# Moving work across three stage seams of a fused two-layer kernel, and four residual additions from VectorE to GpSimd

## The reference, cut to what matters

```
x = x + selective_scan_layer(ln(x))        # ends in a layernorm of its own, with gain and bias
x = x + fp4_gated_ffn(ln(x))
x = x + linear_attention(ln(x))
x = x + fp4_gated_ffn(ln(x))
x = x + forgetting_attention(ln(x))        # 16 heads of 64, decay = cum[t] - cum[s]
x = x + ln(x) @ sign(W).T
x = x + rope_attention(ln(x))              # 16 heads of 8, q and k rotated and normalised
x = x + ln(x) @ sign(W).T
```

## Time and profile before

| | |
|---|---|
| runs of the kernel before | 2290.7, 2298.5, 2292.94 us; median 2292.94 us |
| the profiled execution | 2297.52 us, its span 2295.7 us |
| mean granted TensorE clock | 0.933 of full speed |
| PE busy | 1917.0 us (84% of the span) |
| DVE busy | 1503.1 us (65%) |
| ACT busy | 1379.4 us (60%) |
| GpSimd busy | 1001.4 us (44%) |
| where the four places stand | `prep` 0 to 21 us, `ln_ssm` 364 to 381, `fg` and the start of `fu` 807 to 860, `rp` and the start of `rt` 1908 to 2010 |

### The profile page before, as it was taken

How to read it: one execution, slowest core, us unless ns; L and a number is a source line. 1 busy time by engine, 2 the same in 40 slices (tenths; PEclk the granted TensorE clock), 3 DMA queues, 4 the chain that set the end, 5 groups by cost and what they waited for, 6 DMA issues and landing times. The chain is left out here.

```text
span 2295.7 us, 36184 instructions
## 1 busy us (share of the span) xinstructions
PE 1917.0 (84%) x11875; PEld 885.0 (39%) x11875; DVE 1503.1 (65%) x2277; ACT 1379.4 (60%) x2289; POOL 1001.4 (44%) x1110
## 2 busy tenths in 40 slices
PE   5468885677968748999999999999999767699997
PEld 2123333444654313444444444444444323222222
DVE  5979995793359667787777787777786437311112
ACT  3557773343344336766776667677665435699994
POOL 0167771560136314656666656566656622300001
PEclk9779998798979869999999999999999979799998
DMA  2000000000000011111111112111111101321210
GB/s 91 0 14 0 0 0 1 0 1 1 0 0 1 0 54 47 51 55 51 55 58 58 55 56 57 50 58 59 58 54 63 38 10 37 101 55 46 52 42 37
DMA packets 71431, 84.47 MB, mean 37 GB/s; under 512 B 20544, under 2 KB 44032, under 8 KB 71168
## 3 DMA queue, kind: packets, MB, share of 16 engines
q1 hardware_dynamic: 66224, 79.80, 11.7%
q10 hardware_dynamic: 5040, 2.56, 0.4%
HBM read 71.95 MB, written 9.57 MB: 36 GB/s over the span
## 5 line engine op out<-in xcount | busy, mean ns | idle before, releaser
L1692 DVE SCALAR_TENSOR_TENSOR fu_kv<-fu_ps_kv,fa_vec,fu_kv 128x511 f32<-128x511 f32 x366 | 252.8, 740 | 6.2 <-ACT fu_kv L1622 5.2
L2089 ACT ACTIVATE rt_p<-rt_ps_s 128x1024 f32<-128x1024 f32 x256 | 240.4, 1042 | 26.2 <-PE rt_ps_o L2034 17.4
L1773 POOL TENSOR_TENSOR fu_p<-fu_p 128x768 f32<-128x768 f32 x64 | 116.8, 1824 | 289.2 <-PE fu_ps_n L1467 284.1
L1437 PE MATMUL fu_ps_s<-fu_qn,fu_kn 64*128 64x512 f32 (+3 forms) x1024 | 190.0, 468 | 12.8 <-DVE fu_sg L1738 6.9
L1672 DVE TENSOR_REDUCE fu_nm<-fu_ps_m 128x2 f32<-128x1024 f32 x64 | 78.4, 1225 | 164.9 <-PE fu_ps_m L1460 164.9
L623 POOL TENSOR_TENSOR scan_hC<-scan_h,scan_c 128x1024 f32<-128x1024 f32 x64 | 150.9, 2357 | 71.5 <-DVE scan_h L599 71.5
L1467 PE MATMUL fu_ps_n<-fu_p,fu_vt 128*64 128x512 f32 (+3 forms) x1024 | 166.1, 445 | 0.0
L599 DVE TENSOR_TENSOR_SCAN scan_h<-scan_dA,scan_ps_b 128x1024 f32<-128x1024 f32 x64 | 146.4, 2287 | 2.2
L522 PE MATMUL scan_ps_y<-scan_hC,w_ident 128*128 128x512 f32 x256 | 125.2, 611 | 27.0 <-POOL scan_hC L623 15.4
L2034 PE MATMUL rt_ps_o<-rt_p,rt_va 128*32 128x512 f32 x1024 | 138.1, 611 | 10.0 <-ACT rt_p L2089 8.1
L1495 PE MATMUL fu_ps_kv<-w_XN,fa_wp 128*128 128x512 f32 x244 | 125.7, 639 | 17.6 <-DVE fu_cr L1665 15.4
(11 more groups left out here) (364 smaller groups left out, 5096.0 us busy)
## 6 DMA issues: line engine op xcount, KB each, us to landing
fu_rb<-rms_rows SPq DMA_DIRECT2D x256, 128.0 KB, 2.9
fu_ro<-rms_rows SPq DMA_DIRECT2D x128, 128.0 KB, 2.9
ra_stackq<-rope_parts SPq DMA_DIRECT2D x168, 32.0 KB
ra_stackk<-rope_parts SPq DMA_DIRECT2D x168, 32.0 KB
w_X<-in_xT SPq DMA_DIRECT2D x4, 512.0 KB
fa_wp<-in_wp SPq DMA_DIRECT2D x8, 256.0 KB
fu_cr<-ncum_rows SPq DMA_DIRECT2D x128, 3.0 KB
rope_parts<-rp_hi SPq DMA_DIRECT2D x16, 128.0 KB, 2.4
```

What stands on the lines that cost most here:

```text
L1437: pe.matmul(sps[:, h, at:at + T - t * P], k[head(h), t * P:(t + 1) * P], q[head(h), t * P:T], start=(at == 0), stop=False)
L1692: dve.scalar_tensor_tensor(acc, projected(a, k)[:, 0:T - j], vec[:, a % GA, at:at + 1], acc, ALU.mult, ALU.add).then_inc(done, 1)
L1773: pool.tensor_tensor(tail, tail, P13[:, :, 0:3 * P], ALU.add).then_inc(s.d1, 1)
L2089: act.activation(pr[k % 2][i][:, :, :], sps[(U * n + u) % RING][:, :, :], ACT.Exp, scale=DH_B ** -0.5).then_inc(s.exp, 1)
```

## The change

- `prep`: the 23 later loads are issued by SP, behind its own nine, and no longer by ACT.
- `ln_ssm`: GpSimd adds the residuals of batches 0 to 3; DVE keeps those of batches 4 to 7, and all eight multiplications.
- `fg` and `fu`: the tiles `nc`, `cr` and `mhl` move to the enclosing stage. The 11 memsets are done by DVE in `fg`, behind that of `ones` and ahead of the gates. SP issues the store of `NC` in `fg` as before and waits for it at the start of `fu`. PE, SP and GpSimd no longer wait for the memsets.
- `rp` and `rt`: for the last two batches (`LATE = 2`) the split into three parts moves from `rp` to `rt`. There DVE makes `HI` and `MID`, GpSimd the differences (behind the copies of `va` for batch 0), and SP puts the 12 pieces in DRAM ahead of its loads for batch 1. The tiles `hi`, `mid`, `lo` and `un` move to the enclosing stage.

```diff
@@ prepare_weights @@
                     sp.dma_start(X[:, b:b + 2, :], w.xT_dram[:, b:b + 2, :]).then_inc(s.x, 16)
+                for src, dst in w.loads:
+                    sp.dma_start(dst, src).then_inc(w.loaded, 16)
...
                     act.dma_start(dst, src).then_inc(w.early, 16)
-                for src, dst in w.loads:
-                    act.dma_start(dst, src).then_inc(w.loaded, 16)
@@ ln_ssm @@
                     for n in range(B):
                         scale(n)
-                        if n:
+                        if n > HALF:
                             add(n - 1)
                     add(B - 1)
+
+                @block.gpsimd
+                def _(pool):
+                    for n in range(HALF):
+                        pool.wait_ge(s.norm, n + 1)
+                        pool.tensor_tensor(X[:, n, :], X[:, n, :], DL[:, n, :], ALU.add).then_inc(s.shared, 1)
+                    pool.wait_ge(s.shared, HALF)
@@ forget_gates @@
-                sp.dma_start(ncum_rows, NC[:, :, :]).then_inc(s.put, 16)
-                sp.wait_ge(s.put, 16)
+                sp.dma_start(ncum_rows, NC[:, :, :]).then_inc(held.stored, 16)
...
                 dve.memset(ones[:, :], 1.0).then_inc(s.ones, 1)
+                for k in range(3):
+                    dve.memset(CR[k][:, :], 0.0).then_inc(s.zero, 1)
+                dve.memset(MHL[:, :, :, :], 0.0).then_inc(s.zero, 1)
+                dve.wait_ge(s.zero, 4)
+                for h in range(2):
+                    for k in range(3):
+                        dve.memset(CR[k][64 * h:64 * h + 5, :], 1.0).then_inc(s.made, 1)
+                dve.memset(MHL[:, :, :, 0:3], 1.0).then_inc(s.made, 1)
@@ forget_units @@
                 sp.wait_ge(held.loaded, 16 * (GA + 2))
-                sp.wait_ge(s.set, 9)
-                sp.wait_ge(s.ones, 6)
+                sp.wait_ge(held.stored, 16)
...
                 pe.wait_ge(held.loaded, 16 * (GA + 2))
-                pe.wait_ge(s.set, 9)
-                pe.wait_ge(s.ones, 6)
@@ rope_project @@
-                for n in range(2, B):
+                for n in range(2, SPLIT):
                     put(n, s.put)
-                sp.wait_ge(s.put, 16 * 6 * (B - 1))
+                sp.wait_ge(s.put, 16 * 6 * (SPLIT - 1))
...
-                    if real(older):
+                    if 0 <= older < SPLIT:
                         act.wait_ge(s.un, older + 1)
...
-                for n in range(B):
+                for n in range(SPLIT):
                     pool.wait_ge(s.hi, n + 1)
@@ rope_attend @@
+                    if n == 0:
+                        for k, m in enumerate(late):
+                            for part, (done, tile) in enumerate(((s.hi, HI), (s.mid, MID), (s.lo, LO))):
+                                sp.wait_ge(done, k + 1)
+                                for j in range(2):
+                                    sp.dma_start(parts_dram[part, j, :, m, :], tile[:, j, m, :]).then_inc(s.put, 16)
+                        return
+                    if n == late[0]:
+                        sp.wait_ge(s.put, 16 * 6 * LATE)
...
+                    if i == 0:
+                        for k, m in enumerate(late):
+                            pool.wait_ge(s.hi, k + 1)
+                            pool.tensor_tensor(rest[k][:, :, :], un[m % 2][:, :, :], HI[:, :, m, :], ALU.subtract).then_inc(s.rest, 1)
+                        for k, m in enumerate(late):
+                            pool.wait_ge(s.mid, k + 1)
+                            pool.tensor_tensor(LO[:, :, m, :], rest[k][:, :, :], MID[:, :, m, :], ALU.subtract).then_inc(s.lo, 1)
...
             @block.vector
             def _(dve):
+                for m in late:
+                    dve.tensor_copy(HI[:, :, m, :], un[m % 2][:, :, :]).then_inc(s.hi, 1)
+                for k, m in enumerate(late):
+                    dve.wait_ge(s.rest, k + 1)
+                    dve.tensor_copy(MID[:, :, m, :], rest[k][:, :, :]).then_inc(s.mid, 1)
```

More of the change, by code:

```diff
@@ L33 @@
 ROPE_ROWS = len(ROPE_ORDER) * DH_B
+LATE = 2
 LOAD_FIRST = 16 * 4 * len(ROPE_ORDER)
@@ L1225, in forgetting_attention_stages @@
     with Stage(nc, "fa") as outer:
+        loaded, stored = outer.sems("loaded stored")
         held = named(
-            wp=outer.sb("wp", [P, GA, 4, P]), wo=outer.sb("wo", [P, GA, P]), vec=outer.sb("vec", [P, GA, 3 + 2 * TAPS]), loaded=outer.sems("loaded").loaded,
+            wp=outer.sb("wp", [P, GA, 4, P]), wo=outer.sb("wo", [P, GA, P]), vec=outer.sb("vec", [P, GA, 3 + 2 * TAPS]), nc=outer.sb("nc", [P, KF, T], BF16), cr=[outer.sb(f"cr{k}", [P, T], BF16) for k in range(3)], mhl=outer.sb("mhl", [P, NT, 2, DH_A], BF16),
+            loaded=loaded, stored=stored,
         )
@@ L1237, in forget_gates @@
         ab, e, ln, mn, ng, cum, r1, r2, ones = (st.sb(n, [P, T]) for n in ("ab", "e", "ln", "mn", "ng", "cum", "r1", "r2", "ones"))
-        NC = st.sb("nc", [P, KF, T], BF16)
-        s = st.sems("ones f ab e ln mn ng cum hi r1 mid r2 lo put")
+        NC, CR, MHL = held.nc, held.cr, held.mhl
+        s = st.sems("ones zero made f ab e ln mn ng cum hi r1 mid r2 lo put")
         with st.block() as block:
@@ L1344, in forget_units @@
         QM, KM = st.sb("qm", [P, T], BF16), st.sb("km", [P, T], BF16)
-        CR = [st.sb(f"cr{k}", [P, T], BF16) for k in range(3)]
+        CR, MHL = held.cr, held.mhl
         RR = st.sb("rr", [P, T], BF16)
         nm = st.sb("nm", [P, NT, 2])
-        MHL = st.sb("mhl", [P, NT, 2, DH_A], BF16)
         SG = st.sb("sg", [P, T])
@@ L1355, in forget_units @@
         nps, ssps = st.ps("n", [P, T]), st.ps("ss", [P, T])
-        s = st.sems("set ones kvp tap t1 t2 cv th sk sv vt vc qp qc q2 k2 sa so dsq msq mso fold bits ya yb yc yd y1 ye yf yg yh yi r rb ro put cr0 cr1 cr2 qn kn qm km "
+        s = st.sems("set kvp tap t1 t2 cv th sk sv vt vc qp qc q2 k2 sa so dsq msq mso fold bits ya yb yc yd y1 ye yf yg yh yi r rb ro put cr0 cr1 cr2 qn kn qm km "
                     "mx red hi ml rt rr sc ex pv d1 d2 ds n2 nc gp tg sg gated og wo x")
@@ L1657, in _ @@
             def _(dve):
-                for k in range(3):
-                    dve.memset(CR[k][:, :], 0.0).then_inc(s.set, 1)
-                dve.memset(MHL[:, :, :, :], 0.0).then_inc(s.set, 1)
-                dve.wait_ge(s.set, 4)
-                dve.memset(MHL[:, :, :, 0:3], 1.0).then_inc(s.set, 1)
-                for h in range(2):
-                    for k in range(3):
-                        dve.memset(CR[k][64 * h:64 * h + 5, :], 1.0).then_inc(s.ones, 1)
                 dve.wait_ge(held.loaded, 16 * (GA + 2))
@@ L1823, in rope_attention_stages @@
         stack = [outer.sb(f"stack{n}", [64 + ROPE_ROWS, HEADS_B // 2, T], BF16) for n in "qk"]
+        parts = [outer.sb(n, [P, 2, B, T], BF16) for n in ("hi", "mid", "lo")]
+        un = [outer.sb(f"un{k}", [P, 2, T]) for k in range(2)]
         first = outer.sems("first").first
-        rope_project(nc, w, XN, V, parts_dram, stack, first)
-        rope_attend(nc, w, X, V, parts_dram, stack, first)
+        rope_project(nc, w, XN, V, parts_dram, stack, first, parts, un)
+        rope_attend(nc, w, X, V, parts_dram, stack, first, parts, un)
 def load_stack(sp, stack, parts_dram, n, pairs, sem):
@@ L1836, in load_stack, with rope_project @@
                 sp.dma_start(stack[j][rows, pairs, :], src[e][:, pairs, :]).then_inc(sem, 16)
-def rope_project(nc, w, XN, V, parts_dram, stack, first):
+def rope_project(nc, w, XN, V, parts_dram, stack, first, parts, un):
     with Stage(nc, "rp") as st:
-        HI, MID, LO = (st.sb(n, [P, 2, B, T], BF16) for n in ("hi", "mid", "lo"))
+        HI, MID, LO = parts
+        SPLIT = B - LATE
         mains = [st.ps(f"a{k}", [P, 2, T]) for k in range(2)]
         comps, sums = st.ps("b", [P, 2, T]), st.ps("s", [P, 2, T])
-        rb, rot, un, d1 = ([st.sb(f"{n}{k}", [P, 2, T]) for k in range(2)] for n in ("rb", "rot", "un", "d1"))
+        rb, rot, d1 = ([st.sb(f"{n}{k}", [P, 2, T]) for k in range(2)] for n in ("rb", "rot", "d1"))
         sq, cl, ln = (st.sb(n, [P, 2, T]) for n in ("sq", "cl", "ln"))
@@ L1956, in _, with rope_attend @@
                     pool.tensor_tensor(LO[:, :, n, :], d1[n % 2][:, :, :], MID[:, :, n, :], ALU.subtract).then_inc(s.lo, 1)
-                pool.wait_ge(s.lo, B)
-def rope_attend(nc, w, X, V, parts_dram, stack, first):
+                pool.wait_ge(s.lo, SPLIT)
+def rope_attend(nc, w, X, V, parts_dram, stack, first, parts, un):
     ROWS = ROPE_ROWS
@@ L1979, in rope_attend @@
         tps = fps[:, :].rearrange("p (t a b) -> p t a b", t=NT, a=4)
-        s = st.sems("ones low high va sc exp pv osb t ri ot t2 otc f x")
+        HI, MID, LO = parts
+        rest = [st.sb(f"rest{k}", [P, 2, T]) for k in range(LATE)]
+        late = range(B - LATE, B)
+        s = st.sems("hi rest mid lo put ones low high va sc exp pv osb t ri ot t2 otc f x")
         def batches(step):
```

13 lines of the change are left out of this document (6 added, 7 removed).

## The result

| | before | after |
|---|---|---|
| median of the runs | 2293.52 us (2290.7 to 2298.5, 4 runs) | 2274.76 us (2273.63 to 2275.64, 4 runs) |
| ratio after to before | | 0.9916, 95% interval 0.9898 to 0.9934 |
| profiled execution, its span | 2297.52, 2295.7 us | 2274.57, 2272.7 us |
| mean granted TensorE clock | 0.933 | 0.936 |

The change is 19.3 us faster by the ratio (15.1 to 23.4); forecast were 18.6 and a time of 2274.3. Two numbers agree, and in part by luck: in the first pair of traces `prep` and `ln_ssm` gave 0.9 us less each than forecast, the price in `rt` was set 0.6 too high, and the last stage, which no term has, was 3.5 us shorter. So I go through the four places first.

What follows compares the result with a forecast made beforehand. No engine is busy throughout; each stage begins only when the last engine of the one before ends. Terms 1.8 + 1.2 + 6.6 + 9.0 = 18.6 us less, from 2292.9 to 2274.3 us; range 2267 to 2284.

Steps and rivals of the forecast that it cites:

- the price in `rt`: Start of `rt`: DVE's casts delay GpSimd's memset and copies of `va`; 0.9 us back, between 0 and 2.1.
- The order of ends: `prep`: ACT done early, SP between 15.6 and 17.4, DVE last; PE begins at 19.50, 1.8 us less.
- DVE's end, 18.67: `prep`: DVE's end in the profile before, taken to set PE's start at 19.50 with 0.83 us added.
- The rival in which SP's queue clogs: `prep`: at 1.0 us an issue the next stage begins 8.1 us later than now, total 2284.2 us; chance 0.04.
- The step-by-step collision: `ln_ssm`: DVE's and GpSimd's additions wait for each other; DVE ends at about 379.7, 1.2 us less.
- The no-collision rival: `ln_ssm` and `rt`: engines don't collide, so 2.4 for 1.2 and 9.9 for 9.0 us; total 2272.2; chance 0.12.
- the 0.7 of my chain: `fg`: memsets end at 812.7, moving L1276 there from 811.95; the chain behind it is 0.17 us later.
- the constant 1.06: Seams where SP's wait for a transfer ends last: the next stage's first instruction follows 1.06 us behind.
- waiting for weights: Start of `fu`: PE may wait for the attention's weights, whose last packets move until about 818.4; 5.0 us left.
- The lower bound: `fg` to `fu`: if the wait for weights ended as late as 821.4, 5.0 of the 6.6 us are left.
- a lost head start: Rival in `fu` and `rt`: half of the 6.6 and 2 us come back, total 2279.6 us; chance 0.12.
- The rival in which rope stays at 1.2 GHz: Rope attention: the clock stays low, 0.45 us for each of 256 exponentials pairs, up to 2303 us; chance 0.04.

Runs made afterwards that it cites:

- e3: Kernel before with only the `fg` and `fu` part (memsets in `fg`, store's wait in `fu`); ratio to before 0.9982, median 2290.50 us.
- e7: Changed kernel, but DVE in `ln_ssm` makes all eight multiplications first, then its four additions; one execution, 2269.80 us.
- e10: Changed kernel, but ACT's queue instead of SP's issues the load of the weights `wo` in `fg`; one execution, 2278.20 us.
- e6: Changed kernel, but DVE in the rope attention waits for GpSimd's memset and copies of `va` before its casts; one execution, 2272.34 us.
- e11: Changed kernel with `LATE = 1`: only the last batch is split in the rope attention; one execution, 2271.36 us.
- e4: Kernel before with only the `rp` and `rt` part (splits of batches 6 and 7 moved to `rt`); ratio to before 0.9951, median 2285.04 us.
- e1: Kernel before with only the `prep` part (SP issues the 23 later loads behind X); ratio to before 0.9977, median 2292.11 us.

## Why the prediction was right, point by point

Since single traces scatter, the last column but one takes all traces whose code at that place is the same, from the first matmul of one stage to that of the next (prep from 0):

| place | forecast | the first pair | means over traces (before, after) | why |
|---|---|---|---|---|
| prep | -1.8 | -0.88 | 22.12 to 19.94: -2.2 (5, 7) | DVE ends last, as said; its end, and ACT's before, move from trace to trace |
| `ln_ssm` | -1.2 | -0.3 | 17.98 to 16.77: -1.2 (5, 7) | DVE chain 9.69 to 8.51; the pair's variance matmuls differ by 1.0 |
| `fg` to `fu` | -6.6 | -6.35 | 19.04 to 12.64: -6.4 (5, 7) | the seam took 1.44 (e3 1.33), not 1.06 |
| `rp` to `rt` | -9.9 | -9.84 | 83.32 to 73.44: -9.9 (5, 8) | `un` ends the stage |
| in `rt` | +0.9 | +0.3 | 268.81 to 269.12: +0.3 (5, 6) | casts delay `va` by 0.6, of which 0.3 stay |
| sum | -18.6 | -17.1 | -19.4 | measured -19.3, then -24.3 |

**Prep.** The order of ends was right: SP's last issue came before DVE's end. But it came at 18.19, behind the forecast's 15.6 to 17.4, since the 23 issues took 0.56 us each on average (the first 1.37, the last 0.43); in four of the seven traces it was later than 17.4. The step that was too simple is the one that took DVE's end, 18.67, from one trace as a constant. The constants behind it land between 13.7 and 15.6 us, and of the before traces mine was the earliest. The start before was no constant either: ACT's 35 issues end between 18.66 and 20.12 in the five traces, and mine was again the earliest. So the first pair showed half of the term and the mean a fifth more: on average the start after comes 0.4 us later than forecast and the start before 0.8 us later than in my trace, two errors that partly cancel. The rival in which SP's queue clogs did not come.

**ln_ssm.** The step-by-step collision gave 8.5 us and the trace 8.51; it gave a DVE that goes on at 376.15 and the additions at 1.2 to 1.6. The no-collision rival (7.3 us) is out, by e7 as well. The Trainium skill's rule (SBUF — State Buffer, "SBUF: two separate sides") is that a VectorE instruction with two SBUF inputs and a GpSimd instruction that reads SBUF exclude each other as a whole. The traces agree: 1.44, 1.15 and 1.464 us where they met, 0.68 elsewhere.

**fg and fu.** The memsets lie in `fg` beside DVE's idle time as forecast: L1293 ran at 808.98, 5.24 us behind `fg`'s first matmul, against 4.50 before, the 0.7 of my chain; the rest of the chain began 809.73, 0.1 us later than before. Mis-sized was the constant 1.06: it came from a seam at which SP ended with a wait, and this one ends with an issue, 1.44. I had named waiting for weights as a bound and then as a sign of error. The trace even printed their name; e10 and the steps of the semaphore show that the name misled there, and that in e3 alone the wait was real. The lower bound was no idle one: in the trace before, the last weights landed at 818.94, 0.86 us ahead of the start that I forecast. The 3.3 us of a lost head start are not seen: `fu` to the next stage took 1023.3 to 1030.5 us in all fourteen traces, 1027.5 on average in the five with the old seam and 1028.0 in the nine with the new. With that scatter a loss of 1 us can't be excluded.

**rp and rt.** The end was forecast within 0.1 us. The 0.9 back was a guess between 0 and 2.1, from 1.22 us as the bound of a cast. A cast alone takes 0.68 to 0.69 us; the two together delay the copies by 0.8 and PE by 0.6, and 0.35 of that reaches the stage's length (e6). So the price was too high for two reasons: the cast is shorter than its bound, and not all of PE's delay reaches the end of the stage. The Trainium skill's rule on VectorE's two-port mode and GpSimd (the same page and section) agrees: the cast that met the memset ended 0.55 us behind it, after 2.31 us and not 0.69 (e11). The stage's clock rose a little earlier too. The stretches of 1.5 us of `rt`, before:

```profile
1999.26:2000.76 1.50, 1.50 (x12) 0.29 (x12) 0.00 (x0) 0.93 (x2) 0.00 (x0) 0.62 0.00 0
```

and after:

```profile
1979.58:1981.08 1.50, 1.50 (x16) 0.27 (x12) 1.45 (x2) 0.89 (x2) 0.87 (x2) 0.90 0.00 0
```

Each is the sixth of its stage, 7.5 to 9.0 us behind the first matmul. A granted clock of 0.90 means that four fifths of it ran at 2.4 GHz, and 0.62 one quarter; so the change reached the high clock about 0.8 us earlier, counted from the stage's start. That is not all scatter: the five traces with the old seam have 0.62 to 0.77 in this stretch, the eight with the new seam and two late batches 0.87 to 0.95. The rival in which rope stays at 1.2 GHz is out: the stretches behind this one are at 1.00.

**The sum.** The bounds that I gave add up to 22.7 and not 22.8, which changes nothing.

**What the forecast did not have.** The last stage is 3.4 us shorter in the means (34.84 over four traces without either large seam edit, 31.48 over the seven with both). In all four of the former the clock was low behind the last seam, and in none of the latter. e3 and e4, with one seam each, had 31.1 and 31.5, e11 33.07. That is too regular for an accident of two traces, and it would make the sum 22.7 us, between the two measurements. The changed kernel's nine runs also lie closer together (6.7 us) than the 32 of the kernel before beside e1 to e4 (15.8 us). But for e3 its total speaks against a gain in every execution: its place (6.5 us) and a last stage shorter by 3.7 would make 10.2 us, and its ratio allows 7.8 at most; its trace is that of its fastest run. And nothing shows why: the pause of PE at that seam has the same length in all fourteen traces (2.06 to 2.11 us). It could be an effect of where in time the seam falls, and then another small edit could take it away. This stays open; for the whole change the totals can't decide it, as 3.4 us lie inside their intervals.

## What to carry to other kernels

Find what ends last at a seam, take that end from several traces and not one, and use the seam's constant from a seam that ends in the same way (with an engine's instruction, a wait, or an issue), with a few tenths of doubt. Work moved from VectorE to GpSimd was free here only beside instructions with an input in PSUM. Where both add in SBUF alone, lay out both chains and let each wait for the other's whole instruction, which here gave 8.5 us for 8.51; VectorE's casts in SBUF beside GpSimd paid as well. When the profile names a transfer as what ended a wait, look when its semaphore was complete before you believe it. To judge edits of 1 us in 2300, read the place; the total of 5 to 12 runs told 4 us at best.
